# Moving the masking of gathered features from VectorE to GpSimd in an edge-network kernel

## The reference

```python
w_m = (efeat @ W_msg + b_msg).reshape(E, in_f, -1)
w_a = (efeat @ W_attn + b_attn).reshape(E, in_f, -1)
h_src = feat[src][:, :, None]
e1, e2 = w_m * h_src, w_a * h_src
ex = exp(e2 - segment_max(e2, dst)[dst])
attn = ex / segment_sum(ex, dst)[dst]
ft = segment_sum(e1 * attn, dst).sum(axis=1)
x = layernorm(x + ft)
x = layernorm(x + segment_mean(edge_attr, dst))
```

## Time and profile before

| what | value |
|---|---|
| median of 3 runs, us | 2245.69 |
| lowest and highest run, us | 2245.54, 2249.85 |
| profiled execution: span, us | 2950.2 |
| GpSimd (POOL) busy, instructions | 1687.5 us (57%), 1845 |
| TensorE (PE) busy, instructions | 2137.9 us (72%), 6682 |
| VectorE (DVE) busy, instructions | 1862.0 us (63%), 2907 |
| ScalarE (ACT) busy, instructions | 1256.9 us (43%), 1228 |
| mean granted TensorE clock | 0.861 |

### The profile page before, as it was taken

The page is one execution under the profiler, slowest core; times in us unless marked ns, Lnnn a source line. Parts: engine busy times, 40 slices in busy tenths (PEclk is TensorE's granted clock), DMA queues, the critical chain, the costliest instruction groups (busy, mean ns, idle before and its releaser), DMA issues. The chain is left out here.

```text
span 2950.2 us, 21765 instructions
## 1 busy us (share of the span) xinstructions
PE 2137.9 (72%) x6682; PEld 952.6 (32%) x6682; DVE 1862.0 (63%) x2907; ACT 1256.9 (43%) x1228; POOL 1687.5 (57%) x1845
## 2 busy tenths in 40 slices
PE   2347676676877777877787658877787767887777
PEld 1213233232333333333333223333333323333333
DVE  6246465566666666666676547766667656786776
ACT  3223443434444443454454325444444444554444
POOL 6556355665655565555565465655656565655633
PEclk8658888897988888989888889988989888988988
DMA  6000000000000000000000000000000001001000
GB/s 229 16 10 11 8 12 10 10 10 9 10 9 9 14 10 9 10 14 10 10 13 9 9 10 13 10 12 9 10 12 9 12 9 28 12 8 16 8 2 3
DMA packets 60073, 47.60 MB, mean 16 GB/s; under 512 B 28366, under 2 KB 55439, under 8 KB 59436
## 3 DMA queue, kind: packets, MB, share of 16 engines
q0 software_dynamic: 57632, 29.73, 8.0%
q1 hardware_dynamic: 2316, 16.38, 1.5%
HBM read 44.00 MB, written 1.90 MB: 16 GB/s over the span
## 5 line engine op out<-in xcount | busy, mean ns | idle before, releaser
L652 POOL DMA_INDIRECT AR<-in_xt,AR x1607 | 1538.8, 958 | 974.1 <-DVE AR L1472 491.3
L1128 PE MATMUL PX<-AR,CS 128*128 128x512 f32 x3246 | 1663.7, 642 | 37.8 <-issue 23.9
L1472 DVE CUSTOM_DVE_ANT_1 AR<-PW,AR 128x1024 f32<-128x1024 f32 x815 | 979.6, 1221 | 896.8 <-remote 651.2
L1108 PE MATMUL PW<-WS,LT 100*128 100x512 bf16 x1630 | 549.1, 423 | 683.9 <-DVE AR L1472 511.8
L1128 PEld LDWEIGHTS PX<-AR,CS 128*128 128x128 f32 x3246 | 664.9, 206 | 652.1 <-issue 532.4
L888 ACT ACTIVATE LT<-PTB 100x1024 bf16<-100x1024 bf16 (+1 forms) x221 | 211.2, 956 | 1005.7 <-remote 601.0
L1485 DVE TENSOR_TENSOR AR<-AR,PX 128x1024 f32<-128x1024 f32 (+1 forms) x442 | 501.0, 1134 | 121.3 <-ACT PX L944 76.0
L1108 PEld LDWEIGHTS PW<-WS,LT 100*128 100x128 bf16 x1630 | 141.5, 103 | 1113.7 <-DVE AR L1472 543.2
L946 ACT ACTIVATE AR<-AR 128x2048 f32<-128x2048 f32 (+1 forms) x221 | 412.9, 1869 | 7.2
L950 ACT ACTIVATE PX<-AR 128x1024 f32<-128x1024 f32 (+1 forms) x221 | 212.4, 961 | 412.3 <-DVE AR L1485 294.8
L944 ACT ACTIVATE PX<-AR 128x1024 f32<-128x1024 f32 (+1 forms) x221 | 231.0, 1045 | 39.4 <-DVE AR L1485 30.1
(11 more groups left out here) (192 smaller groups left out, 517.7 us busy)
## 6 DMA issues: line engine op xcount, KB each, us to landing
AR<-in_xt,AR POOLq DMA_INDIRECT x1607
AR<-in_eat SPq DMA_DIRECT2D x3, 3128.0 KB
AR<-in_eat SPq DMA_DIRECT2D x1, 3120.0 KB
y_d<-AR SPq DMA_DIRECT2D x1, 784.0 KB
AR<-y_d SPq DMA_DIRECT2D x1, 784.0 KB
AR<-in_es,E0I POOLq DMA_INDIRECT x48
y_d<-AR POOLq DMA_INDIRECT x36
CS<-in_cst SPq DMA_DIRECT2D x1, 442.0 KB, 5.3
```

The costliest lines, as they stand in the source:

```text
L652: g.indirect_dma_start(feat(h, j - j0, j - j0 + 1), None, xt, bass.IndirectOffsetOnAxis(ap=node, axis=0)).then_inc(hg_sem(h), 16)
L1108: i = pe.matmul(PAIRS[s % 2][:, j, :], LT[:, g % 3, lo:lo + 128], WS[:, :], start=True, stop=True)
L1128: i = pe.matmul(PDR, IDN, x, start=(a == 0 and j == 0), stop=(g == LAST[k] and j == n - 1))
L1472: v.tensor_tensor_reduce(em(g, j, j + 2).rearrange("p (x c) -> p x c", c=32), w, hb, 1.0, LOW, ALU.mult, ALU.max, accum_out=MXC[:, k % 2, ...
```

## The change

The masking of gathered features for all blocks but the first goes from VectorE to GpSimd. There it is done group by group, behind the gathers of the following group, with two instructions in place of a share of one: the features times the mask, then plus a floor that is now 0 or 1 (1 for an empty slot). The mask therefore has two buffers. `mult` waits for GpSimd's sum in place of VectorE's maximum, and `valid(k)` waits for GpSimd to be through with block k - 2. A gather no longer waits for a whole older group: ahead of every second slot it waits for the pair that used the same place last. The limit of three blocks ahead is gone. The first block's five groups keep their floors on VectorE, as product and sum.

```diff
-    over = [h for h, lo, m in held if lo < at + n and at < lo + m] + [LAST[k - 4]] * (k >= 4)
+    over = [h for h, lo, m in held if lo < at + n and at < lo + m]
...
+PLACE, PREV = {}, []
+for g, j in PAIR:
+    PREV.append(PLACE.get(FAT[g] + j, -1))
+    PLACE[FAT[g] + j] = FROM[g] + j // 2
...
             def gather(k, h):
                 j0, n = GRP[h][1:3]
                 for j in range(j0, min(j0 + n, CAPS[k])):
+                    user = PREV[FROM[h] + (j - j0) // 2]
+                    if (j - j0) % 2 == 0 and user >= 0:
+                        g.wait_ge(S["v_mult"], user + 1)
...
                     for h in range(FIRST[k] + (k == 1), LAST[k] + 1):
-                        if FOLD[h] is not None:
-                            g.wait_ge(S["v_mult"], FROM[FOLD[h] + 1])
                         if h == FIRST[k] + 1 and k + 1 < NC:
                             runs_of(k + 1)
                         gather(k, h)
+                        if h > FIRST[1]:
+                            floors(h - 1)
+
+                def floors(h):
+                    k, j0, n, a = GRP[h]
+                    g.wait_ge(hg_sem(h), hg_count(h))
+                    if h == FIRST[k]:
+                        g.wait_ge(S["v_ev"], k + 1)
+                    x = feat(h).rearrange("p (j i) -> p j i", i=16)
+                    g.tensor_tensor(x, x, VLD[:, k % 2, j0:j0 + n].unsqueeze(2).broadcast_to([128, n, 16]), ALU.mult)\
+                     .then_inc(S["g_ml"], 1)
+                    g.wait_ge(S["g_ml"], h - LAST[0])
+                    g.tensor_tensor(x, x, FLR2[:, k % 2, j0:j0 + n].unsqueeze(2).broadcast_to([128, n, 16]), ALU.add)\
+                     .then_inc(S["g_fl"], 1)
...
+                floors(NGR - 1)
...
                 def valid(k):
                     d = DEG[k]
-                    if k >= 2:
-                        v.wait_ge(S["v_hm"], HMS[LAST[k - 2]])
+                    if k == 2:
+                        v.wait_ge(S["v_hm"], LAST[0] + 1)
+                    if k > 2:
+                        v.wait_ge(S["g_fl"], LAST[k - 2] - LAST[0])
...
-                    link(v.tensor_scalar(FLR2[:, k % 2, 0:d], VLD[:, 0:d], LOW, 1.0, ALU.mult, ALU.add))
+                    link(v.tensor_scalar(FLR2[:, k % 2, 0:d], VLD[:, k % 2, 0:d], -1.0, 1.0, ALU.mult, ALU.add))
...
                     if j == 0:
-                        v.wait_ge(S["v_hm"], HMS[g])
+                        if k == 0:
+                            v.wait_ge(S["v_hm"], g + 1)
+                        else:
+                            v.wait_ge(S["g_fl"], g - LAST[0])
...
-                    if nx is not None:
-                        k = GRP[nx][0]
-                        if k in (0, NC - 1):
-                            floors(nx, nx + 1)
-                        elif nx == FIRST[k]:
-                            for seg in SEGS:
-                                if GRP[seg[0]][0] == k:
-                                    floors(seg[0], seg[-1] + 1)
+                    if nx is not None and nx <= LAST[0]:
+                        floors(nx)
```

More of the change, by code:

```diff
@@ L348, in gnn_kernel @@
         XP = reg([128, roff[1] + max(DEG[1::2]), K], bf16)
-        VLD = reg([128, BINS])
+        VLD = reg([128, 2, BINS])
         FLR2 = reg([128, 2, BINS])
@@ L397, in gnn_kernel @@
             a_w a_T a_exp a_mc a_dn a_z a_u a_r a_m a_ex a_fx
-            g_m g_b d_sc d_x a_sq p_sq p_c p_v v_nrm a_x a_p a_out d_y d_yl d_yz v_xm d_xg v_ys d_ou v_ad""".split()
+            g_m g_b g_ml g_fl d_sc d_x a_sq p_sq p_c p_v v_nrm a_x a_p a_out d_y d_yl d_yz v_xm d_xg v_ys d_ou v_ad""".split()
         S = {n: sem(n) for n in names}
@@ L412, in gnn_kernel @@
         d_hl = [sem(f"d_hl{a}") for a in range(LAST[NC - 1] - FIRST[NC - 1] + 1)]
-        d_h = [sem(f"d_h{i}") for i in range(4)]
+        d_h = [sem(f"d_h{i}") for i in range(2)]
         d_wr = [S["d_wr"], sem("d_wa"), sem("d_wb")]
@@ L433, in hg_sem @@
             k, j0, n, a = GRP[g]
-            return d_h0[a] if k == 0 else d_hl[a] if k == NC - 1 else d_h[k % 4]
+            return d_h0[a] if k == 0 else d_hl[a] if k == NC - 1 else d_h[g % 2]
         def hg_count(g):
@@ L439, in hg_count @@
                 return 16 * min(n, CAPS[k] - j0)
-            return 16 * sum(CAPS[x] for x in range(1, k + 1) if x % 4 == k % 4)
+            return 16 * sum(min(GRP[h][2], CAPS[GRP[h][0]] - GRP[h][1]) for h in range(FIRST[1], g + 1) if h % 2 == g % 2)
         def em(g, lo=0, hi=None):
@@ L675, in runs_of @@
                         g.wait_ge(S["a_p"], 4 * (k - 3) + 3)
-                        for h in range(FIRST[k - 3], LAST[k - 3] + 1):
-                            g.wait_ge(hg_sem(h), hg_count(h))
+                        if k == 3:
+                            for h in range(LAST[0] + 1):
+                                g.wait_ge(hg_sem(h), hg_count(h))
                     edges_of(k, E0I[:, k:k + 1])
@@ L911, in first @@
                         a.wait_ge(S["p_T"], LAST[k - 2] + 1)
-                    a.activation(part(k, 99, 100)[:, 1:d, :], VLD[:, 1:d].unsqueeze(2), ACT.Relu, bias=1.0, scale=-1.0).then_inc(S["a_p"], 1)
+                    a.activation(part(k, 99, 100)[:, 1:d, :], VLD[:, k % 2, 1:d].unsqueeze(2), ACT.Relu, bias=1.0, scale=-1.0).then_inc(S["a_p"], 1)
                     h = upper(edge(k))
@@ L1426, in valid @@
                     d = DEG[k]
-                    if k >= 2:
-                        v.wait_ge(S["v_hm"], HMS[LAST[k - 2]])
+                    if k == 2:
+                        v.wait_ge(S["v_hm"], LAST[0] + 1)
+                    if k > 2:
+                        v.wait_ge(S["g_fl"], LAST[k - 2] - LAST[0])
                     if k >= 1:
                         v.wait_ge(S["a_p"], 4 * (k - 1) + 1)
-                    link(v.tensor_scalar(VLD[:, 0:d], IOTA[:, 0:d], DEGR[:, k:k + 1], None, ALU.is_lt))
-                    link(v.tensor_scalar(FLR2[:, k % 2, 0:d], VLD[:, 0:d], LOW, 1.0, ALU.mult, ALU.add))
+                    link(v.tensor_scalar(VLD[:, k % 2, 0:d], IOTA[:, 0:d], DEGR[:, k:k + 1], None, ALU.is_lt))
+                    link(v.tensor_scalar(FLR2[:, k % 2, 0:d], VLD[:, k % 2, 0:d], -1.0, 1.0, ALU.mult, ALU.add))
                     v.wait_ge(d_xe[k % 3], 16 * (k // 3 + 1))
-                    v.tensor_tensor(edge(k), edge(k), VLD[:, 0:d].unsqueeze(2).broadcast_to([128, d, 16]), ALU.mult)\
+                    v.tensor_tensor(edge(k), edge(k), VLD[:, k % 2, 0:d].unsqueeze(2).broadcast_to([128, d, 16]), ALU.mult)\
                      .then_inc(S["v_ev"], 1)
@@ L1448, in low, with floors @@
                     v.tensor_tensor(part(k, 32, 48), x, upper(x), ALU.subtract).then_inc(S["v_x3"], 1)
[L1450 to L1458, removed]
+                def floors(g):
+                    k, j0, n, a = GRP[g]
+                    v.wait_ge(hg_sem(g), hg_count(g))
+                    if g == 0:
+                        v.wait_ge(S["v_ev"], 1)
+                    h = feat(g).rearrange("p (j i) -> p j i", i=16)
+                    link(v.tensor_tensor(h, h, VLD[:, 0, j0:j0 + n].unsqueeze(2).broadcast_to([128, n, 16]), ALU.mult))
+                    v.tensor_tensor(h, h, FLR2[:, 0, j0:j0 + n].unsqueeze(2).broadcast_to([128, n, 16]), ALU.add)\
                      .then_inc(S["v_hm"], 1)
@@ L1594, in regular @@
                 mean(0)
-                floors(0, 1)
+                floors(0)
                 for i in range(NST):
```

## The result

The changed kernel takes **2434.95 us** (median of 4 runs, 2434.33 to 2435.07) and the kernel before 2245.61 (2244.35 to 2249.85). The ratio is 1.0841 with a 95% interval of [1.0827, 1.0854], so the change made the kernel slower by 189 us.

The account below looks back on a forecast made before the run. GpSimd's queue was taken as the bound; 2245.7 + 235 (floors) + 6 (ports) + 1 (mask's wait) = 2487 us, range 2407 to 2575.

Parts of the forecast that it names:

- The bound: GpSimd's queue bounds a run from the first blocks on; rival that it is not the bound: chance 0.09.
- the standstills of the earlier trace: "Remote" waits at line 1472, 651 us together, were taken as belonging to the recorded execution, not to a run.
- Remote waits still there: The changed kernel's profile was expected to show "remote" waits again.
- The sum of the kernel before: GpSimd's queue added up without waits: 2111 + 4 + 119 = 2234 us, against a run of 2245.7.
- The price of a floor: Product and sum added to GpSimd's queue per group: 1.12 us each, 235 us over 210 groups, between 178 and 281.
- Ports: GpSimd's new arithmetic meeting VectorE's two-operand instructions: 11 us, less 5 given back, net +6.
- The return: Line 1458's floors leaving VectorE disturb fewer GpSimd gathers: 5 us given back.
- VectorE's 36.7 us of floors: Floors taken off VectorE were worth nothing on the path; a gain of 37 if VectorE were the bound.
- Places: Feature places given back by the pair, without the limit of three blocks: taken as 0, between 0 and 12 us.
- Waits of VectorE: In a run VectorE was said to wait at `valid` for edges; no size given.
- The mask's wait: GpSimd waiting for VectorE's mask at a block's first group: 1 us, 0 to 12; rival at about 2730, chance 0.03.
- Configuration at each turn: Rival: GpSimd configured anew at each of 420 turns between DMA and arithmetic, 13 to above 10,000 us; chance 0.02.

Follow-up runs that it names:

- experiment 1: The kernel before, unchanged, recorded a second time: 2246.41 us.
- 4: The kernel after with GpSimd's product with the mask issued twice: 2538.41 us.
- 5: The kernel before, floors still on VectorE, with an unused product and sum on a spare tile behind each group's gathers on GpSimd: 2445.43 us.
- 9: The kernel after without the gathers of the seventh and eighth slot of the groups of eight: 2144.32 us; the kernel before, cut the same way, 2151.35.
- the earlier trace: The first recording of the kernel before, nothing changed, used for the prediction: span 2950.2 us.
- 6: The kernel before with each of VectorE's 71 floors done twice: 2254.05 us.
- 2: The kernel before with only places given back by the pair and no limit of three blocks, floors still on VectorE: 2246.27 us.
- E0I: Not a run: an operand name in the profile rows of GpSimd's edge transfers; the text does not define it and gives no run time.
- 7: The kernel after with GpSimd's product alone, its sum left out: 2314.69 us.
- 3: The kernel after with the old waits for places by the group, so only the floors moved to GpSimd: 2436.68 us.
- 10: The kernel after with the product behind the fourth gather of the next group and the sum behind the fifth: 2386.62 us.

## Why the prediction was right, and where not

**The bound** was right. GpSimd's queue is what a run waits for: no gap over 0.31 us (experiment 1), each added instruction paid in full (4, 5), nothing paid once the queue is shorter (9). I took the standstills of the earlier trace rows for something of the recording; they belonged to that one execution. "Remote waits still there" was therefore wrong.

**The sum of the kernel before** came within 12 us of a run, partly because two errors cancel. The stretch that I put at 2005 us takes 2027, mostly since a gather is 0.956 us on average and not the 0.944 of an undisturbed one (18 us). It starts at 89.27 and not at 105.90. From the issue of the last edge transfer to the end it takes 128 us, where I had 4 + 119. That the sum came so close is in part luck.

**The price of a floor is the step that was mis-sized**: 1.12 us a group as predicted, 0.883 measured, 235 us against 186. The mechanism held, and the range (2407 to 2575) held the time. Its terms:

| us a group | predicted | measured |
|---|---|---|
| gap ahead of the product | 0.08 | 0.02 |
| product, gap, sum | 0.85 | 0.413 + 0.078 + 0.394 = 0.885 |
| gap behind the sum, in place of one gap | 0.33 - 0.30 | 0.252 - 0.304 |
| longer transfers | 0.156 | 0.03 |

The arithmetic read from the earlier trace rows was good to 4%. What failed is the use of the earlier trace rows: one indirect transfer behind a dependent product, 0.33 late and 1.10 us long, taken as the rule. That transfer wrote to DRAM what the product had made, and had to wait for it. A gather does not wait for the sum ahead of it, and 128 of the 210 transfers behind a sum are gathers: one starts 0.15 late and takes 0.98, as the timeline after shows. Of 49 us of error these two terms make 44 (0.082 + 0.127, times 210).

**Ports**: +11 - 5 was predicted. Of the 420 new instructions in the stretch 13 took over 0.5 us, together some 5 us more than usual. The return is not visible: 47 gathers over 1.05 us in the stretch before, 48 after. Of the 49 such gathers that the second recording has from 89 us to the end, 46 ran beside line 1434, 1441, 1448, 1458 or 1505, as the earlier trace rows had suggested. Such company does not always lengthen a gather: 261 gathers ran beside a VectorE instruction with two SBUF operands, and 48 of these were over 1.05 us, against 1 of the 1300 others. The Trainium skill (SBUF — State Buffer, Who interferes with whom) has a VectorE instruction with two SBUF inputs contend with GpSimd instructions that read SBUF and not with those that only write; the trace agrees if an indirect gather, which fetches its row numbers, counts as reading.

**VectorE's 36.7 us of floors** at 0 on the path: right, within the 10 us of experiments 5 and 6. **Places** at 0: right (2).

**Waits of VectorE**: that it waits at `valid` for edges was wrong for the kernel before. There it waited at line 1458 for landings, and the last block's edge product came 7 us behind its transfer's issue without waiting. This is the last block's edge product before the change, behind the transfer issued at 2116.43:

```profile
2123.87 0.53 DVE L1434 TENSOR_TENSOR AR<-AR 128x352 f32<-128x352 f32 x1
```

After the change it is true, 72.2 us at line 1451. The last block shows it; GpSimd's edge transfer, then VectorE's edge product:

```profile
2300.89 0.98 POOL L658 DMA_INDIRECT AR<-in_es,E0I  x1 [0.34 <-issue]
```

```profile
2304.07 0.53 DVE L1451 TENSOR_TENSOR AR<-AR 128x352 f32<-128x352 f32 x1 [2.97 <-DMA AR<-in_es,E0I]
```

**The mask's wait**: 1 us predicted. GpSimd waited for it once, 0.67 us, at the first floor, which also ran long (1.07 us):

```profile
88.20 1.02 POOL L658 DMA_INDIRECT AR<-in_es,E0I  x1 [0.30 <-issue]
...
98.26 0.96 POOL L653 DMA_INDIRECT AR<-in_xt,AR  x1 [0.30 <-issue]
99.90 1.07 POOL L697 TENSOR_TENSOR AR<-AR 128x128 f32<-128x128 f32 x1 [0.67 <-DVE AR L1451]
101.05 0.40 POOL L700 TENSOR_TENSOR AR<-AR 128x128 f32<-128x128 f32 x1
```

It is not harmless everywhere: in experiment 9, where GpSimd is no longer the bound, its floors waited 59.2 us for the mask, in 14 waits.

**Configuration at each turn** falls. The two configuration instructions of the earlier trace rows have moved to the first product, and stay two. By line:

```profile
L697 POOLq MODIFY_POOL_CONFIG  x2: 32/32/32, 99.2 to 99.3; - x2
```

From 99.3 to the first product at 99.90 are 0.6 us, most of them the mask's wait, and behind none of the 210 sums in the stretch does the next transfer start more than 1.20 us later. The Trainium skill (GPSIMD Engine Reference, Instruction dispatch) gives about 6 us for the first call of newly loaded code; no such time shows here.

## What to carry to other kernels

Before a wait in a profile is believed, add up the busiest queue without any wait and compare the sum with the time of a run: it showed the bound here although the recorded execution was odd. Work that moves onto an engine whose queue is the bound lengthens the time, here by 0.34 to 0.57 us for an instruction of 0.4, even if the engine that it leaves is the busier one by the page, and how far the time falls when that queue is shortened (94 us here) says when this ends. Where arithmetic must share a queue with transfers, put a transfer between two dependent instructions, and none with several waits right behind the second: the two together took back 48 of 189 us.

## What the runs showed of the hardware

On GpSimd a gather behind a gather starts 0.30 us after its end, arithmetic behind a gather 0.02, and a gather behind arithmetic 0.15 to 0.16. A short instruction among gathers thus costs less than its own duration: 0.34 us for one of 0.41 (7). I had expected it to cost more. Behind a sum that waits for its product the next transfer starts later the more waits stand in front of it, at the median 0.15 us with one, 0.32 with two, 0.39 with three and 0.45 with four. That preparing the next transfer overlaps arithmetic would explain it, and that a sum that waits for its product takes away part of the time for it; this reading fits 3, 5, 7 and 10 but was not tried by itself.
